# First stage of a two-layer LoRA network: products with gathered rows in four row quarters of the array

## The chip, the cores and the metric

One core of one Trainium2 chip runs the whole network as a single program. The metric is the device time of one execution in microseconds. It is 992.07 us before the change (median of 3 runs, 991.67 to 992.74).

## What is computed

The input x has 128 sequences of 32 tokens with 512 features, so 4,096 tokens. Two layers follow one another, each adding to x. The change lies in the first half of the first layer, a dense product with a low-rank correction (LoRA) whose factors are picked per sequence by a slot number:

```python
base_out = jnp.einsum('bti,oi->bto', x, W) + b
A = lora_As[adapter_mapping]          # per sequence, 512 x 16
Bm = lora_Bs[adapter_mapping]         # per sequence, 16 x 512
lora_h = jnp.einsum('bti,bir->btr', x, A)
lora_out = jnp.einsum('btr,bro->bto', lora_h, Bm)
return base_out + lora_out * SCALING
```

What it returns goes through a gated feed-forward block (gate, up and down weights with 1,376 hidden features), and the second layer is again of dense products with low-rank corrections. All arithmetic is in float32.

## The kernel before

**Arithmetic.** A float32 product is made of three products of a reduced type (`fp32r`): each operand is split into a high part (written by ACT) and a low part (the rest, written by DVE), and `mm3` (L1822) issues high x high, high x low and low x high into the same accumulator. Each of these is one weight load (128 columns) and one matmul.

**Stages.** Stage 1 (to about 149 us of the span) makes the output c of the code above in 8 tiles (`t`, NT = 8) of 512 tokens, and stores it to a scratch tensor. Stage 2 (to about 782 us) is the feed-forward block, and the rest is the second layer. The engines run programs written out by hand, each in a fixed order, and wait for each other on semaphores. PE's program for stage 1 is at the end of `pe_program`.

**One tile of stage 1 on PE.** The 512 output features are four blocks of 128 (`m`), each with a PSUM bank `acc[m]` of 128 features x 512 tokens. The 512 input features are four blocks (`k`).
- `cond_base(t, m, k)` is the dense product of block k into bank m: three matmuls over 512 tokens. A tile has 16 of them.
- `turn_a(t)` transposes the gathered factors A: a tile has 16 sequences in two groups (`g`, NG = 2) of 8 sequences, that is of 8 x 16 = 128 gathered rows and 256 tokens. Eight transposes go into two banks of the ring. ACT and DVE split them into `a_hi` and `a_lo` (`turn_a` of their programs, L955 and L1396).
- `lora_in(t)` multiplies x by them, 24 matmuls of 256 tokens, into one ring bank with 128 rows (sequence, rank). DVE masks the result (`h_masked`, L1410: `own_batch` leaves, of each sequence's 16 rows, only its own 32 tokens), ACT makes `lh_hi` (L967), and DVE `lh_lo` (L1416).
- `cond_lora(t, m)` multiplies the masked rows by the gathered factors B (`b_hi`, `b_lo`) and adds to bank m: for each of the two groups three matmuls with all 128 rows over 256 tokens. It closes the bank: its last matmul counts `pe_acc` up by one, ACT's `close_c` (L973) adds the bias, writes `c_out` and counts `c_closed`, and the next tile's first product into that bank waits for this.

The order on PE in tiles 1 to 7 is: base of bank 0, `turn_a`, base of bank 1, `lora_in`, base of banks 2 and 3, then `cond_lora` of banks 0 to 3. In tile 0 the dense products go block by block as the weights arrive, `lora_in` stands ahead of the last four of them, and the rest is the same.

**Around it.** In a tile ACT works in this order: `a_hi`, `b_hi`, `xa_hi` of the next tile, `lh_hi`, then four times `close_c` with a piece `dt` of the down weights behind it (tiles 0 to 5), or splits of the operands of stage 2 (`cop`, tiles 6 and 7). DVE's order is `a_lo`, `b_lo`, `xa_lo` of the next tile, `h_masked`, `lh_lo`, `dt` or `cop` work. Stage 2 begins with products into banks 0 and 2, which wait for `c_closed` of tile 7; behind them a product waits for ACT's copy of a bank (L1041).

Of the kernel before, what the change touches and what calls it, by code (L numbers as in the profile page):

```python
# [10 lines left out]
P = 128  # L11
# [13 lines left out]
def plain(ap):  # L25
    return ap.bitcast(F32)


def build(nc, x, slots, langs, w0, b0, ab_table, w_gate, w_up, w_down, wb1, rhs2, ra1, b2t, b1, out):
    NT, KC, _, _ = x.shape  # L30
# [8 lines left out]
    GT = GB * SEQ  # L39
    NG = TOK // GT  # L40
    E = P // R
# [54 lines left out]
    w0_hi = work("w0_hi", [KC, D], F32R)  # L96
# [193 lines left out]
    warm_done = sem("warm_done")  # L290
# [37 lines left out]
    def nth(t, m=KC - 1):  # L328
        return t * KC + m + 1
# [1045 lines left out]
    def dve_program(e):  # L1375
# [287 lines left out]
        e.memset(plain(warm[:, :]), 0.0).then_inc(warm_done, 1)  # L1663
# [154 lines left out]
    def pe_program(e):  # L1818
# [41 lines left out]
        def cond_base(t, m, k):  # L1860
            mm3(acc[m][:, :], w0_hi[:, k, m * P:(m + 1) * P], w0_lo[:, k, m * P:(m + 1) * P],
                xa_hi[t % 2][:, k, :], xa_lo[t % 2][:, k, :], k == 0, False)

        def cond_lora(t, m):
            s = t % 2
            for g in range(NG):
                tok = slice(g * GT, (g + 1) * GT)
                done = mm3(acc[m][:, tok], b_hi[s][:, g, m * P:(m + 1) * P], b_lo[s][:, g, m * P:(m + 1) * P],
                           lh_hi[s][:, tok], lh_lo[s][:, tok], False, g == NG - 1)
            done.then_inc(pe_acc, 1)  # L1870
# [188 lines left out]
        e.wait_ge(warm_done, 1)  # L2059
        for _ in range(9):  # L2060
            mm(ring[3][:, :], warm[:, 0:P], warm[:, :], True, True)
        for k in range(KC):
            e.wait_ge(x_lo, nth(0, k))
            e.wait_ge(w0_lo_done, k + 1)
            if k == 2:
                turn_a(0)
            if k == 3:
                lora_in(0)
            for m in range(KC):
                cond_base(0, m, k)  # L2070
        for t in range(NT):
            for m in range(KC):
                if t > 0:
                    e.wait_ge(c_closed, nth(t - 1, m))
                    for k in range(KC):
                        if m == 0:
                            e.wait_ge(x_lo, nth(t, k))
                        cond_base(t, m, k)
                    if m == 0:
                        turn_a(t)  # L2080
                    if m == 1:
                        lora_in(t)
            e.wait_ge(lh_lo_done, t + 1)
            e.wait_ge(b_lo_done, NG * (t + 1))
            for m in range(KC):
                cond_lora(t, m)
# [131 lines left out]
```

## Time and profile before

| | us |
|---|---|
| median of 3 runs | 992.07 (991.67 to 992.74) |
| profiled execution, its own time | 994.31 |
| its span | 992.6 |
| PE busy, share of the span | 982.7, 99% |
| DVE, ACT, POOL busy | 586.8, 464.9, 256.0 |
| DMA, mean over the span | 232 GB/s |

The span runs from the first to the last instruction. The profiled execution took 994.31 us, 2.2 us above the median of the runs shown. PE's busy time says little by itself, because a matmul's record is longer than the distance to the next one; the rows are read by the starts of neighbouring instructions.

### The profile page before, as it was taken

To read this page: it belongs to the slowest core of one execution; us is meant where nothing else is said; L and a number is where in the kernel's file an instruction comes from. 1 tells how busy PE (TensorE), PEld (TensorE's weight loads), DVE (VectorE), ACT (ScalarE), POOL (GpSimd) and SP (SyncE) were. 2 spreads that over 40 slices of the span, in tenths; PEclk is the share of its full clock that TensorE was granted. 3 is DMA by queue.
4 is the path that set the end of the run, shared out by engine and by line. 5 is a ranking of instruction groups with operands and counts; after the bars stand their busy time and mean duration, and the time that the engine had idled before them with its cause. 6 is when DMAs were issued, how large, how long until landed. Compare 5 with 4: busy or idle time off the path is not lost.

```text
span 992.6 us, 14042 instructions
## 1 busy us (share of the span) xinstructions
PE 982.7 (99%) x4787; PEld 830.4 (84%) x4787; DVE 586.8 (59%) x969; ACT 464.9 (47%) x854; POOL 256.0 (26%) x244
## 2 busy tenths in 40 slices
PE   9999999999999999999999999999999999999998
PEld 7888888878888888888888888888888998888876
DVE  5654586777784323596423398333377587785762
ACT  4645567555661333572333373233356273535342
POOL 5242232654400631400532230261140450000000
PEclk9999999999999999999999999999999999999999
DMA  8997866666977877867887777986688740615222
GB/s 287 334 327 281 309 216 245 240 231 236 340 265 260 283 229 193 274 222 267 287 278 193 233 249 248 321 279 192 192 293 285 254 166 28 228 61 194 78 93 85
DMA packets 121486, 230.12 MB, mean 232 GB/s; under 512 B 12612, under 2 KB 12612, under 8 KB 121160
## 3 DMA queue, kind: packets, MB, share of 16 engines
q1 hardware_dynamic: 118880, 220.81, 66.5%
q0 software_dynamic: 2400, 8.41, 2.3%
q8 instruction: 39, 0.64, 0.3%
q14 instruction: 31, 0.25, 0.1%
q10 hardware_dynamic: 136, 0.01, 0.0%
HBM read 165.74 MB, written 63.44 MB: 231 GB/s over the span
## 4 chain that ended last, share of the span: by engine, by line
PE 96%; DVE 1%; ACT 1%; issue 1%; DMA 0%; SPq 0%; ACTq 0%; DVEq 0%
PE bank L1820 95%; PE bank L1844 1%; PE bank L1981 1%; DMA w_raw<-in_w 0%; ACT xs_hi L1126 0%; ACT bank L1277 0%; DVE hg L1644 0%; DVE t_lo L1535 0%; DVE greater L1624 0%; ACT res L1285 0%; DVE diff L1601 0%; DVE top L1597 0%; DVE wins L1620 0%; DVE rank L1627 0%; DVE greater L1618 0%
## 5 line engine op out<-in xcount | busy, mean ns | idle before, releaser
L1820 PE MATMUL bank<-cop_hi,wring 128*128 128x512 f32 x1234 | 380.8, 389 | 0.9 <-ACT bank L1041 0.9
L1820 PEld LDWEIGHTS bank<-cop_hi,wring 128*128 128x128 f32 x1234 | 231.8, 188 | 49.4 <-ACT bank L1041 1.3
L1820 PE MATMUL bank<-cop_lo,wring 128*128 128x512 f32 x616 | 239.8, 389 | 0.0
L1820 PE MATMUL bank<-op_hi,wring 128*128 128x512 f32 x560 | 173.8, 389 | 0.0
L1472 DVE TENSOR_TENSOR v<-bank,p7s 128x512 f32<-128x512 f32 x44 | 30.4, 692 | 204.6 <-PE bank L1820 204.6
L1820 PEld LDWEIGHTS bank<-cop_lo,wring 128*128 128x128 f32 x616 | 115.7, 188 | 23.8
L1820 PEld LDWEIGHTS bank<-op_hi,wring 128*128 128x128 f32 x560 | 105.2, 188 | 21.7
L1820 PE MATMUL bank<-op_lo,wring 128*128 128x512 f32 x280 | 109.0, 389 | 0.0
L1072 ACT ACTIVATE s<-bank 128x512 f32<-128x512 f32 x44 | 26.3, 598 | 117.9 <-PE bank L1820 117.8
L1458 DVE TENSOR_TENSOR op_lo<-h,op_hi 128x512 fp32r<-128x512 f32 x100 | 72.9, 747 | 3.3 <-ACT op_hi L1029 3.1
L821 POOL TENSOR_TENSOR h_t<-h,h 128x512 f32<-128x512 f32 x20 | 27.7, 1385 | 161.1 <-DVE h L1494 161.1
L1029 ACT ACTIVATE op_hi<-h 128x512 fp32r<-128x512 f32 x100 | 62.7, 627 | 13.6 <-PE bank L1820 12.7
L1820 PEld LDWEIGHTS bank<-op_lo,wring 128*128 128x128 f32 x280 | 52.6, 188 | 10.9
L1041 ACT ACTIVATE bank<-bank 128x512 f32<-128x512 f32 x44 | 25.6, 582 | 76.7 <-PE bank L1820 76.7
L860 POOL TENSOR_TENSOR t_sum<-x_second,x_second 128x256 f32<-128x256 f32 x12 | 8.9, 780 | 177.3 <-DMA x_second<-x_scratch 177.3
L1820 PE MATMUL bank<-xa_hi,w_hi 128*128 128x512 f32 x128 | 51.6, 404 | 0.8 <-DVE w_lo L1389 0.8
L1820 PE MATMUL bank<-xa_lo,w_hi 128*128 128x512 f32 x128 | 50.8, 397 | 0.0
L1820 PE MATMUL bank<-xa_hi,w_lo 128*128 128x512 f32 x128 | 50.5, 395 | 0.0
L1477 DVE TENSOR_TENSOR p7s<-bank,p7s 128x512 f32<-128x512 f32 x44 | 30.4, 691 | 25.0 <-PE bank L1820 24.9
L1063 ACT ACTIVATE s<-bank 128x512 f32<-128x512 f32 x44 | 26.3, 599 | 30.6 <-PE bank L1820 30.6
L1048 ACT ACTIVATE p7s<-bank 128x512 f32<-128x512 f32 x44 | 26.3, 598 | 29.9 <-PE bank L1820 29.9
L776 POOL DMA_INDIRECT ab<-in_ab_table,row_i x16 | 18.7, 1171 | 81.9 <-DVE b_lo L1400 75.8
(227 smaller groups left out, 1931.4 us busy)
## 6 DMA issues: line engine op xcount, KB each, us to landing
wring<-wgu_scratch SPq DMA_DIRECT2D x231, 256.0 KB, 3.1
wring<-wd_scratch SPq DMA_DIRECT2D x140, 256.0 KB, 4.9
wgu_scratch<-wring SPq DMA_DIRECT2D x77, 256.0 KB, 3.5
x_raw<-in_x SPq DMA_DIRECT2D x32, 256.0 KB, 6.2
c_scratch<-c_out SPq DMA_DIRECT2D x32, 256.0 KB, 2.9
c<-c_scratch SPq DMA_DIRECT2D x32, 256.0 KB, 4.6
xs_raw<-x_scratch SPq DMA_DIRECT2D x16, 512.0 KB, 6.2
out<-res SPq DMA_DIRECT2D x32, 256.0 KB, 2.1
```

What stands on the lines that cost most here:

```text
L776: e.indirect_dma_start(out=ab[g][:, :], out_offset=None, in_=ab_table, in_offset=bass.IndirectOffsetOnAxis(ap=row_i[:, col:col + 1], axis= ...
L821: e.tensor_tensor(h_t3[p][:, :], h22[p][:, :], h12[p][:, :], ALU.subtract).then_inc(t3_done, 1)
L1029: e.activation(op_hi[n % N_OP][:, :], op_source[i][p][:, :], ACT.Copy).then_inc(op_hi_done, 1)
L1041: e.activation(bank_y[b][:, :], bank_a[b][:, :], ACT.Copy).then_inc(ay_done, 1)
L1048: e.activation(p7s[b][:, :], bank_w[b][:, :], ACT.Copy).then_inc(p7s_done, 1)
L1063: e.activation(s1[j % 2][:, :], bank_a[j % 2][:, :], ACT.Silu).then_inc(silu1_done, 1)
L1072: e.activation(s2[j % 2][:, :], bank_z[j % 2][:, :], ACT.Silu).then_inc(silu2_done, 1)
L1458: e.tensor_tensor(op_lo[n % N_OP][:, :], op_source[i][p][:, :], plain(op_hi[n % N_OP][:, :]), ALU.subtract).then_inc(op_lo_done, 1)
L1472: e.tensor_tensor(v[b][:, :], bank_z[b][:, :], p7s[b][:, :], ALU.add).then_inc(gc22_done, 1)
L1477: e.tensor_tensor(p7s[b][:, :], bank_y[b][:, :], p7s[b][:, :], ALU.add).then_inc(gc21_done, 1)
L1820: return e.matmul(out_ap, lhs, rhs, start=start, stop=stop, skip_group_check=True)
L1844: done = e.transpose(bank[:, k * P:(k + 1) * P], ab[g][:, k * P:(k + 1) * P], ident[:, :])
```

## The change

The mask leaves most of `cond_lora`'s products zero: of the 128 rows of a group, the 32 rows of a quarter (two sequences) meet only their own 64 tokens. The changed `cond_lora` multiplies only these. One matmul of 128 rows by 256 tokens becomes four of 32 rows by 64 tokens, each on its own quarter of the array's rows. The four that stand in a row write to four different banks: in turn 0 quarter i writes to bank i, in turn 1 to bank i + 1 and so on, and after four turns each quarter has been in each bank. A tile has 4 turns x 2 groups x 3 products x 4 quarters = 96 small matmuls. A turn waits, by the new semaphore `pe_turn`, until the turn before is complete, and three dense matmuls (`cond_base` of block k = 3) stand between two turns. All four banks close together, at the end of the last dense product, which counts `pe_acc` up by four. `turn_a` moves to the tile's head, and `lora_in` to just before bank 3 (in tile 0 all four last dense products, which stood behind `lora_in`, are now among the turns). The warm-up's semaphore is replaced by `dve_chain`, to make room for `pe_turn`.

```diff
+    PART = 32
+    NPART = P // PART
+    PT = GT // NPART
...
-    warm_done = sem("warm_done")
+    pe_turn = sem("pe_turn")
...
-        e.memset(plain(warm[:, :]), 0.0).then_inc(warm_done, 1)
+        linked(e.memset(plain(warm[:, :]), 0.0))
...
-            mm3(acc[m][:, :], w0_hi[:, k, m * P:(m + 1) * P], w0_lo[:, k, m * P:(m + 1) * P],
-                xa_hi[t % 2][:, k, :], xa_lo[t % 2][:, k, :], k == 0, False)
-
-        def cond_lora(t, m):
-            s = t % 2
-            for g in range(NG):
-                tok = slice(g * GT, (g + 1) * GT)
-                done = mm3(acc[m][:, tok], b_hi[s][:, g, m * P:(m + 1) * P], b_lo[s][:, g, m * P:(m + 1) * P],
-                           lh_hi[s][:, tok], lh_lo[s][:, tok], False, g == NG - 1)
-            done.then_inc(pe_acc, 1)
+            return mm3(acc[m][:, :], w0_hi[:, k, m * P:(m + 1) * P], w0_lo[:, k, m * P:(m + 1) * P],
+                       xa_hi[t % 2][:, k, :], xa_lo[t % 2][:, k, :], k == 0, k == KC - 1)
+
+        def cond_lora(t, turn):
+
+
+            s, own = t % 2, KC // NPART
+            if turn == 0:
+                e.wait_ge(lh_lo_done, t + 1)
+                e.wait_ge(b_lo_done, NG * (t + 1))
+            else:
+                e.wait_ge(pe_turn, (NPART - 1) * t + turn)
+            for c in range(own):
+                for g in range(NG):
+                    for b_, h_ in ((b_hi[s], lh_hi[s]), (b_hi[s], lh_lo[s]), (b_lo[s], lh_hi[s])):
+                        for i in range(NPART):
+                            m = (i + turn) % NPART * own + c
+                            rows, tok = slice(i * PART, (i + 1) * PART), slice(g * GT + i * PT, g * GT + (i + 1) * PT)
+                            done = mm(acc[m][:, tok], b_[rows, g, m * P:(m + 1) * P], h_[rows, tok], False, False)
+            if turn + 1 < NPART:
+                done.then_inc(pe_turn, 1)
...
-        for k in range(KC):
-            e.wait_ge(x_lo, nth(0, k))
-            e.wait_ge(w0_lo_done, k + 1)
-            if k == 2:
-                turn_a(0)
-            if k == 3:
-                lora_in(0)
-            for m in range(KC):
-                cond_base(0, m, k)
         for t in range(NT):
-            for m in range(KC):
-                if t > 0:
+            if t == 0:
+                for k in range(KC):
+                    e.wait_ge(x_lo, nth(0, k))
+                    e.wait_ge(w0_lo_done, k + 1)
+                    if k == 2:
+                        turn_a(0)
+                    if k == KC - 1:
+                        lora_in(0)
+                    else:
+                        for m in range(KC):
+                            cond_base(0, m, k)
+            else:
+                turn_a(t)
+                for m in range(KC):
                     e.wait_ge(c_closed, nth(t - 1, m))
-                    for k in range(KC):
+                    if m == KC - 1:
+                        lora_in(t)
+                    for k in range(KC - 1):
                         if m == 0:
                             e.wait_ge(x_lo, nth(t, k))
                         cond_base(t, m, k)
-                    if m == 0:
-                        turn_a(t)
-                    if m == 1:
-                        lora_in(t)
-            e.wait_ge(lh_lo_done, t + 1)
-            e.wait_ge(b_lo_done, NG * (t + 1))
-            for m in range(KC):
-                cond_lora(t, m)
+
+            cond_lora(t, 0)
+            for m in range(KC - 1, 0, -1):
+                cond_base(t, m, KC - 1)
+                cond_lora(t, KC - m)
+            cond_base(t, 0, KC - 1).then_inc(pe_acc, KC)
```

Where the order on PE moves (names with numbers are buffers; in the shapes, the columns are those of the output). First place, tile 0, from the last products of `lora_in` on. Before:

```order
L1820 MATMUL bank<-xa_hi_68,a_lo 128x256
L1820 MATMUL bank<-xa_hi_68,w_hi 128x512
L1820 MATMUL bank<-xa_lo_70,w_hi 128x512
L1820 MATMUL bank<-xa_hi_68,w_lo 128x512
L1820 MATMUL bank<-xa_hi_68,w_hi 128x512
L1820 MATMUL bank<-xa_lo_70,w_hi 128x512
L1820 MATMUL bank<-xa_hi_68,w_lo 128x512
```

Six more such dense matmuls follow, then `cond_lora`'s first, with its wait for `lh_lo_done`. Changed, the same place:

```order
L1824 MATMUL bank<-xa_hi_68,a_lo 128x256
L1824 MATMUL bank<-lh_hi_64,b_hi_60 128x64 x4
L1824 MATMUL bank<-lh_lo_66,b_hi_60 128x64 x4
L1824 MATMUL bank<-lh_hi_64,b_lo_62 128x64 x4
L1824 MATMUL bank<-lh_hi_64,b_hi_60 128x64 x4
L1824 MATMUL bank<-lh_lo_66,b_hi_60 128x64 x4
L1824 MATMUL bank<-lh_hi_64,b_lo_62 128x64 x4
L1824 MATMUL bank<-xa_hi_68,w_hi 128x512
```

The twelve dense matmuls that stood between `lora_in` and the products that need its result have moved behind the first of them.

Second place, tile 1, the end of `lora_in` and the first turns, with the waits. In the kernel before, `lora_in` is followed by 24 dense matmuls (banks 2 and 3). Changed, nine are left:

```order
162 L1824 MATMUL bank<-xa_hi_69,w_hi 128x512
...
170 L1824 MATMUL bank<-xa_hi_69,w_lo 128x512
171 L1824 MATMUL bank<-lh_hi_65,b_hi_61 128x64 [waits b_lo_done,lh_lo_done]
172 L1824 MATMUL bank<-lh_hi_65,b_hi_61 128x64 x3
173 L1824 MATMUL bank<-lh_lo_67,b_hi_61 128x64 x4
174 L1824 MATMUL bank<-lh_hi_65,b_lo_63 128x64 x4
175 L1824 MATMUL bank<-lh_hi_65,b_hi_61 128x64 x4
176 L1824 MATMUL bank<-lh_lo_67,b_hi_61 128x64 x4
177 L1824 MATMUL bank<-lh_hi_65,b_lo_63 128x64 x4
178 L1824 MATMUL bank<-xa_hi_69,w_hi 128x512
179 L1824 MATMUL bank<-xa_lo_71,w_hi 128x512
180 L1824 MATMUL bank<-xa_hi_69,w_lo 128x512
181 L1824 MATMUL bank<-lh_hi_65,b_hi_61 128x64 [waits pe_turn]
```

Third place, the border between tiles 0 and 1. Before, the products of `cond_lora` that close bank 3 are followed at once by the dense products of tile 1, whose first waits for `c_closed` of bank 0. Changed:

```order
104 L1824 MATMUL bank<-xa_hi_68,w_hi 128x512
105 L1824 MATMUL bank<-xa_lo_70,w_hi 128x512
106 L1824 MATMUL bank<-xa_hi_68,w_lo 128x512
107 L1848 MATMUL bank<-ident,ab_54 128x128 [waits ab_in0]
108 L1848 MATMUL bank<-ident,ab_54 128x128 x3
109 L1848 MATMUL bank<-ident,ab_55 128x128 [waits dve_freed,ab_in1]
110 L1848 MATMUL bank<-ident,ab_55 128x128 x3
111 L1824 MATMUL bank<-xa_hi_69,w_hi 128x512 [waits x_lo,c_closed]
```

The eight transposes have moved ahead of the first dense product, between the closing of the four banks and the wait for the first of them. On DVE, ACT, POOL and SP the order is the same in both kernels.

## Rows read from the trace of the kernel before

**Rows 1.** The page: busy time, the chain that ended last, one costly group.
```profile
PE 982.7 (99%) x4787; PEld 830.4 (84%) x4787; DVE 586.8 (59%) x969; ACT 464.9 (47%) x854; POOL 256.0 (26%) x244
...
PE bank L1820 95%; PE bank L1844 1%; PE bank L1981 1%; DMA w_raw<-in_w 0%; ACT xs_hi L1126 0%; ACT bank L1277 0%; DVE hg L1644 0%; DVE t_lo L1535 0%; DVE greater L1624 0%; ACT res L1285 0%; DVE diff L1601 0%; DVE top L1597 0%; DVE wins L1620 0%; DVE rank L1627 0%; DVE greater L1618 0%
...
L1820 PE MATMUL bank<-xa_hi,w_hi 128*128 128x512 f32 x128 | 51.6, 404 | 0.8 <-DVE w_lo L1389 0.8
```

The last of these reads: count, busy us, mean ns of one, idle us of PE just before them and what ended it.

**Rows 2.** Chain of waits in stage 1, tile 1: start us, us, what.
```profile
28.86 0.87 PE bank L1844 x8
29.73 16.73 PE bank L1820 x96
```

**Rows 3.** Timeline of PE, tile 1: start us, us, engine, line, op, tile.
```profile
35.21 0.40 PE L1820 MATMUL bank<-xa_hi,w_hi 128*128 128x512 f32 x1
...
40.45 0.39 PE L1820 MATMUL bank<-xa_hi,w_lo 128*128 128x512 f32 x1
40.67 0.28 PE L1820 MATMUL bank<-lh_hi,b_hi 128*128 128x256 f32 x1
...
43.43 0.28 PE L1820 MATMUL bank<-lh_hi,b_lo 128*128 128x256 f32 x1
43.55 0.40 PE L1820 MATMUL bank<-xa_hi,w_hi 128*128 128x512 f32 x1
```

**Rows 4.** Weight loads and matmuls by tile: duration ns min/median/max, first and last start.
```profile
L1820 PEld LDWEIGHTS bank<-warm x9: 287/330/333, 1.5 to 4.7; 128*128 128x128 f32 x9
L1820 PE MATMUL bank<-warm x9: 628/628/794, 1.5 to 5.1; 128*128 128x512 f32 x9
L1820 PEld LDWEIGHTS bank<-cop_hi,wring x1234: 186/188/192, 149.0 to 728.3; 128*128 128x128 f32 x177
```

**Rows 5.** Timeline of PE, tile 0, the first matmul behind `lora_in`.
```profile
20.31 0.40 PE L1820 MATMUL bank<-xa_hi,w_hi 128*128 128x512 f32 x1
```

**Rows 6.** Timeline of DVE, tiles 0 and 1.
```profile
20.51 0.69 DVE L1410 SCALAR_TENSOR_TENSOR h_masked<-bank,own_batch 128x512 f32<-128x512 f32 x1 [1.72 <-PE bank L1820]
21.90 0.94 DVE L1416 TENSOR_TENSOR lh_lo<-h_masked,lh_hi 128x512 fp32r<-128x512 f32 x1 [0.70 <-ACT lh_hi L967]
...
29.96 1.29 DVE L1396 TENSOR_TENSOR a_lo<-bank,a_hi 128x512 fp32r<-128x512 f32 x2 [0.82 <-ACT a_hi L955]
...
32.37 2.49 DVE L1385 TENSOR_TENSOR xa_lo<-x_raw,xa_hi 128x512 fp32r<-128x512 f32 x4
35.41 0.69 DVE L1410 SCALAR_TENSOR_TENSOR h_masked<-bank,own_batch 128x512 f32<-128x512 f32 x1 [0.55 <-PE bank L1820]
36.80 0.69 DVE L1416 TENSOR_TENSOR lh_lo<-h_masked,lh_hi 128x512 fp32r<-128x512 f32 x1 [0.70 <-ACT lh_hi L967]
```

**Rows 7.** Chain of waits, second layer: what a long wait of PE ended with.
```profile
958.46 0.69 DVE res L1552
```

**Rows 8.** Timeline of PE at the same place.
```profile
959.19 0.50 PE L1820 MATMUL bank<-t_hi,s_hi 128*128 128x512 f32 x1 [1.93 <-DVE res L1552]
959.53 0.40 PE L1820 MATMUL bank<-t_lo,s_hi 128*128 128x512 f32 x1
959.76 0.40 PE L1820 MATMUL bank<-t_hi,s_lo 128*128 128x512 f32 x1
```

**Rows 9.** Timeline of ACT, tile 1.
```profile
41.59 0.69 ACT L973 ACTIVATE c_out<-bank,b 128x512 f32<-128x512 f32 x1 [4.82 <-PE bank L1820]
...
45.44 0.64 ACT L1000 ACTIVATE dt<-ds 128x512 fp32r<-128x512 f32 x1
```

**Rows 10.** Timeline of DVE, tiles 6 and 7.
```profile
124.73 1.15 DVE L1416 TENSOR_TENSOR lh_lo<-h_masked,lh_hi 128x512 fp32r<-128x512 f32 x1 [0.70 <-ACT lh_hi L967]
...
141.38 0.69 DVE L1436 TENSOR_TENSOR c_t<-c,c 128x512 f32<-128x512 f32 x1 [1.03 <-DMA c<-c_scratch]
```

**Rows 11.** Timeline of ACT, start of stage 2.
```profile
149.88 1.14 ACT L1014 ACTIVATE cop_hi<-c 128x512 fp32r<-128x512 f32 x2
150.92 0.59 ACT L1041 ACTIVATE bank<-bank 128x512 f32<-128x512 f32 x1
```

More of the change, by code:

```diff
@@ L2057, in out_h2 @@
                 False, True).then_inc(pe_acc, 1)
-        e.wait_ge(warm_done, 1)
+        e.wait_ge(dve_chain, 1)
         for _ in range(9):
             mm(ring[3][:, :], warm[:, 0:P], warm[:, :], True, True)
-        for k in range(KC):
-            e.wait_ge(x_lo, nth(0, k))
-            e.wait_ge(w0_lo_done, k + 1)
-            if k == 2:
-                turn_a(0)
-            if k == 3:
-                lora_in(0)
-            for m in range(KC):
-                cond_base(0, m, k)
-        for t in range(NT):
-            for m in range(KC):
-                if t > 0:
+        for t in range(NT):
+            if t == 0:
[12 more added lines that the diff above has]
+                for m in range(KC):
                     e.wait_ge(c_closed, nth(t - 1, m))
-                    for k in range(KC):
+                    if m == KC - 1:
+                        lora_in(t)
+                    for k in range(KC - 1):
                         if m == 0:
```

## The prediction

> **What bounds the kernel.** I read the page first: PE is busy 99% of the span, and its matmuls make 95% of the chain that ended last [rows 1]. Before the 128 first products of the dense blocks, all of them in stage 1, PE idled 0.8 us, once, for the first weights [rows 1]. The chain of waits says the same of one tile: eight transposes (0.87 us) and 96 matmuls (16.73 us), and nothing between [rows 2]. So a tile takes 17.60 us without a wait, and two things count: what PE no longer streams, and what PE now waits for. Third I read PE's timeline by its starts. Dense matmuls of 512 columns start about 0.227 us apart (24 of them from 35.21 to 40.67), those of 256 columns 0.120 us apart, and the 24 of `cond_lora` take 43.55 - 40.67 = 2.88 us a tile [rows 3], 23.0 us in 8 tiles. That is all that the change can win. It would need PE not to lose it elsewhere. Last I read ACT and DVE for what feeds `cond_lora`.
>
> **The small matmuls.** Removed: 24 matmuls of 256 columns, 2.88 us a tile. Added: 96 of 64 columns and 32 rows, in 24 rounds of four. No such instruction is in the trace, so their price is bounded. From the two distances [rows 3] 256 columns cost 0.107 us and a matmul 0.013 us on top; four at once, bound by their columns alone, would be 64 columns and one fixed part, 0.027 + 0.013 = 0.040 us a round, 0.96 us a tile. At the other end nothing overlaps. The nearest row to a short matmul with a load of its own is a transpose, 128 columns, eight in 0.87 us or 0.109 us each [rows 2]; 96 of those are 10.4 us a tile. Between these ends I ask what a weight load takes. Its record is 330 ns while the matmul's is 628 and 188 when that is about 389 [rows 3, 4], so it gives back 142 ns where the matmul of 512 columns gives back 239. Half the clock costs 512 columns 213 ns; some 26 ns of the 239 are other than columns, and the load has 142 - 26 = 116 ns of array time when fast (an estimate from these rows), as if its 128 columns went through twice. So behind a matmul of 256 columns the load is just covered, and behind one of 64 columns it isn't. If the loads of the four quarters run side by side, a round takes one load, about what a 256-column matmul takes now. I take 0.120 us a round: 24 x 0.120 = 2.88 us, **no gain at all**, with 0.96 and 10.4 us as ends.
>
> The Trainium skill (TensorE: Matmul & The Clock Gate, LDWEIGHTS) says that a load takes its columns divided by 1.2 in ns, and that 32 rows by 128 columns take as long as 128 by 128. By that, an estimate, a round is 0.107 us and the kernel would stand 2.5 us lower than my sum.
>
> **Changing between quarters and whole array.** A tile has four turns, so eight changes, 64 in all. A dense matmul's record is 0.39 us against a distance of 0.227 us [rows 3]: 0.16 us of each lies under its successor. If this overlap is lost at a change, it costs 0.16 us; if not, nothing. Eight first changes fall into the wait below. I take 56 x 0.16 = **+9.0 us**, with 0 as the other end. This is the second thing that no row shows.
>
> The Trainium skill (TensorEngine Tiling, Key Properties) has a rule against the change here: changing the tiling mode drains the array. It gives no price; by it 0.16 us stands, without it the sum is 9.0 us less.
>
> **The wait for `lh_lo`.** `lora_in`'s result goes through DVE, ACT, DVE. In tile 0 the next matmul after `lora_in` starts at 20.31 [rows 5], and `lh_lo` ends at 21.90 + 0.94 = 22.84 [rows 6]. Twelve dense matmuls (2.72 us) covered this, and now stand behind it. A wait costs some 0.14 us beyond its releaser: DVE's `res` ended at 959.15 [rows 7], PE's next record began at 959.19, and the distance to the one behind it was 0.34 us in place of 0.227 [rows 8]. So PE stands still 2.53 + 0.14 = **+2.7 us**, once. In tiles 1 to 7 nine dense matmuls are left, 2.04 us. From the start behind `lora_in` (35.21) to the end of `lh_lo` (37.49) are 2.28 us [rows 3, 6]: 0.24 + 0.14, and some 0.05 us more because DVE itself is only just ready. With T as the end of the tile before on PE's stream: ACT closes four banks with four `dt` in about 4.5 us [rows 9], DVE's `a_lo` can start at T + 5.3 (one `a_hi` lies between), from there to its last `xa_lo` are 4.9 us [rows 6], so DVE is free at T + 10.2; PE ends `lora_in` at T + 9.95 (0.87 + 6.12 + 2.88, and 0.1 from below). I count 0.45 us for tiles 1 to 5, **+2.3**; 0.9 for tile 6, where `lh_lo` took 1.15 us and not 0.69; and 1.3 for tile 7, where DVE waits for a transfer first [rows 10]: **+2.2**.
>
> **Banks that close together.** The closing starts 0.2 us after T and takes 0.69 us [rows 9], so bank 0 is free at T + 0.9. The transposes, moved ahead, cover 0.87 us of it: 0.1 us at each of 7 borders, **+0.7**. The other banks are freed before PE asks, 2 us apart. At the start of stage 2 no transposes stand there: **+1.0**. There ACT also makes two `cop_hi` (1.14 us) between the closings and the copy that the third product waits for [rows 11]. They end at T + 3.8, the copy at T + 4.4, PE asks at T + 3.75: **+0.7**. `pe_turn` costs nothing: the three dense matmuls between (0.68 us) cover the 0.28 us that a record takes.
>
> The transposes need only their gathered rows, asked for a tile ahead. DMA, POOL and SP have the same list and slack.
>
> **Sum.** 0 (small matmuls) + 9.0 (changes) + 2.7 + 2.3 + 2.2 + 0.7 + 1.0 + 0.7 (waits, 9.6) = +18.6 us. The profiled execution goes from a span of 992.6 to 1011.2. It took 994.31 us, 2.2 above the median; on the median of 992.07 the forecast is 1010.7, **1011 us**.
>
> **Rival A: the quarters run side by side and their loads are short.** If a load of 32 rows takes a quarter of a full one, or several are held ready, a round is 0.040 us and a tile saves 2.88 - 0.96 = 1.92 us, 15.4 in 8. Less waits of 9.6: -5.8, 986 us if changes cost nothing, and 995 us with them. This is the case on the faster side. It decides at 0.070 us a round with free changes. For it: the four of a round use other rows and other banks. Against it: the load record in [rows 4]. The Trainium skill (TensorEngine Tiling, Key Properties) says that different tiles load and multiply in parallel; no row here shows it, and by it either the forecast or this rival holds.
>
> **Rival B: the quarters don't overlap.** Each small pair costs what a transpose costs, 0.109 us. Then 96 x 0.109 = 10.5 us a tile in place of 2.88, +60.7 in all, and with the waits +70: 1062 us, 1071 with the changes. For it: the transposes, the shortest pairs there are, stand no closer than 0.109 us [rows 2]. Against it: none there had another quarter to go to. This is also the case in which the change doesn't do what it says.
>
> **Rival C: PE falls to its slow clock in the wait of tile 0.** Matmul records of 628 ns mark it [rows 4]. Against it: after 1.93 us of idling the next record was 0.50 us, with 0.40 behind it [rows 8], so the fast level held. It would add some us and change no sign; I fold it into the others.
>
> **Chances.** Forecast, a round between 0.09 and 0.20 us and all in all 1000 to 1030 us: 0.50. Rival A: 0.27, of it 0.22 faster, 0.03 no difference, 0.02 slower. Rival B: 0.23. Two in a thousand, 2 us, is about what a measurement can tell from no change. So faster 0.22, same 0.04 (0.01 from the forecast's edge), slower 0.74. The forecast's case alone spans 1000 to 1030. The range reaches down to rival A with free changes, 985, and up to rival B without them, 1063; what lies above 1063 and some of A below 985 is left out, about 0.2.
>
> **What would show it.** In the changed profile: starts of the 128x64 matmuls 0.03 us apart on average (rival A: 0.01, rival B: 0.11); a turn of 24 taking 0.7 us and the distance to the dense matmul behind it 0.16 longer than its pattern; PE waiting once for 2.5 us or so for DVE L1420 in tile 0 and about 0.4 in the others, and for ACT L977 at the borders. Tiles would be 17.6 + 1.1 + 0.6 = 19.3 us. The prediction is wrong if a turn takes below 0.3 us or above 2 us, or if the wait for `lh_lo` doesn't show.

## The result, and the profile after

| | before | changed |
|---|---|---|
| median of 4 runs each | 992.40 us (991.67 to 994.35) | **1024.01 us** (1021.68 to 1025.88) |
| profiled execution, its own time | 994.31 | 1021.68 |
| its span | 992.6 | 1020.0 |

The ratio is 1.0316 (1.0292 to 1.0341): the change costs 3.2%, 31.6 us on the medians and 27.4 us between the two profiled spans. The forecast was 1011 us. The sign and the range held, its own case (no gain at all from the small matmuls) is what came, and 13 us are missing from its sum on the medians, 8.8 us between the profiled spans (1011.2 against 1020.0).

The page of the changed kernel, with the lines that answer to [rows 1], and the row of PE's granted clock:

```profile
span 1020.0 us, 15201 instructions
PE 1004.0 (98%) x5363; PEld 836.0 (82%) x5363; DVE 586.9 (58%) x969; ACT 463.3 (45%) x854; POOL 255.3 (25%) x244
...
PEclk9799997999999999999999999999999999999999
```

576 matmuls more than in [rows 1], still 98% busy, and two slices of the 40 (each 25.5 us) at about three quarters of the clock. The kernel before has a mean granted clock of 1.000 in its profiled execution, the changed one 0.987. Cut at the places where the dense matmuls change their pace (columns: window, length, PE, PEld, DVE, ACT, POOL busy with counts, granted clock, DMA share, GB/s):

```profile
23.00:37.00 14.00, 14.00 (x99) 10.75 (x98) 2.54 (x4) 4.18 (x8) 4.49 (x4) 0.51 0.61 235
37.00:164.00 127.00, 123.43 (x1110) 100.69 (x1108) 66.21 (x107) 60.14 (x118) 31.69 (x28) 1.00 0.75 266
166.00:181.00 15.00, 14.22 (x97) 10.47 (x94) 7.48 (x15) 6.13 (x14) 4.32 (x4) 0.54 0.25 91
181.00:1020.00 839.00, 832.30 (x3932) 698.24 (x3930) 495.72 (x823) 379.41 (x696) 203.97 (x188) 1.00 0.68 221
```

There are two stretches at about half clock (the 1.2 GHz level), in windows of 14 and 15 us, and the other two windows have a granted clock of 1.00 (the 2.4 GHz level). Each begins just behind the two long waits for `lh_lo`, in tile 0 and in tile 7. PE's timeline in tile 0:

```profile
21.75 0.30 PE L1824 MATMUL bank<-lh_hi,b_hi 32*128 32x64 f32 x4 [2.17 <-DVE lh_lo L1420]
...
23.10 0.59 PE L1824 MATMUL bank<-xa_hi,w_lo 128*128 128x512 f32 x1
...
24.07 0.40 PE L1824 MATMUL bank<-lh_hi,b_lo 32*128 32x64 f32 x4
24.29 0.40 PE L1824 MATMUL bank<-lh_hi,b_hi 32*128 32x64 f32 x4
...
36.76 0.42 PE L1824 MATMUL bank<-xa_hi,w_hi 128*128 128x512 f32 x1
```

A dense record grows from 0.39 to 0.6 us and a round of four from 0.11 to 0.21 us (24.07 to 24.29). The first slow dense record starts 1.35 us after the wait ended (21.75 to 23.10), the first fast one again at 36.76, 13.7 us later.

**One turn at full clock**, in tile 1. First PE, then its weight loads:

```profile
48.15 0.40 PE L1824 MATMUL bank<-xa_hi,w_lo 128*128 128x512 f32 x1
48.47 0.30 PE L1824 MATMUL bank<-lh_hi,b_hi 32*128 32x64 f32 x4
48.61 0.28 PE L1824 MATMUL bank<-lh_lo,b_hi 32*128 32x64 f32 x4
...
49.05 0.28 PE L1824 MATMUL bank<-lh_hi,b_lo 32*128 32x64 f32 x4
49.26 0.50 PE L1824 MATMUL bank<-xa_hi,w_hi 128*128 128x512 f32 x1
49.60 0.39 PE L1824 MATMUL bank<-xa_lo,w_hi 128*128 128x512 f32 x1
```

```profile
48.47 0.19 PEld L1824 LDWEIGHTS bank<-lh_hi,b_hi 32*128 32x128 f32 x4 [0.36 <-issue]
48.58 0.19 PEld L1824 LDWEIGHTS bank<-lh_lo,b_hi 32*128 32x128 f32 x4
```

The four of a round are so close that the view shows them as one row ("x4"), matmuls and loads alike, and the next four follow 0.11 us later. So the quarters do run side by side, and a round still takes 0.112 us, about what the forecast gave one load (0.116), against the 0.120 us of the 256-column matmul that it replaces [rows 3]. The edges can be read off too: dense to quarter 0.32 us (48.15 to 48.47) where dense to dense is 0.227, the first round 0.14, quarter to dense 0.21 (49.05 to 49.26), and then 0.34 to the second dense matmul. Over the undisturbed distances (0.227 and 0.112) that is 0.12 us on the way to the quarters and 0.21 us on the way back.

**One tile**, by the chain of waits in tiles 2 and 3 (answers to [rows 2]):

```profile
65.09 0.72 DVE lh_lo L1420
...
65.86 6.82 PE bank L1824 x108
```

`lh_lo` stands on the path in every tile now, where the chain before had matmuls alone. And what PE waited for, in all (us, times, longest):

```profile
PE bank L1824 <- DVE lh_lo L1420: 5.3, 3, 2.6
```

The list of waits shows idle time only beyond a matmul's record, which is why five tiles with a shorter wait are not in it. In starts:

```profile
65.34 0.39 PE L1824 MATMUL bank<-xa_hi,w_lo 128*128 128x512 f32 x1
65.86 0.30 PE L1824 MATMUL bank<-lh_hi,b_hi 32*128 32x64 f32 x4
```

These are 0.52 us in place of 0.227: 0.29 us more (0.26 to 0.29 in the five tiles), of which some 0.09 us are the change to the quarters, which costs as much where nothing is waited for (0.32 above).

### The profile page after: what moved, and what is told of

Its sections match the earlier page's. It is cut to its first block, busy times and chain, and to the rows that moved or that the text cites. A ratio compares the mean times of both kernels' runs of the same rounds, so it can differ in the third digit from the quotient of the medians.

```text
span 1020.0 us, 15201 instructions
## 1 busy us (share of the span) xinstructions
PE 1004.0 (98%) x5363; PEld 836.0 (82%) x5363; DVE 586.9 (58%) x969; ACT 463.3 (45%) x854; POOL 255.3 (25%) x244
## 4 chain that ended last, share of the span: by engine, by line
PE 92%; DVE 3%; ACT 2%; DMA 1%; issue 1%; POOL 0%; SPq 0%; ACTq 0%; DVEq 0%
PE bank L1824 90%; DMA ab<-in_ab_table,row_i 1%; PE bank L1996 1%; PE bank L1848 1%; DVE lh_lo L1420 1%; DVE h_masked L1414 1%; ACT lh_hi L971 1%; DMA c<-c_scratch 0%; ACT xs_hi L1130 0%; ACT c_out L977 0%; DMA slot_i<-in_slots 0%; DVE xa_lo L1389 0%; DVE cop_lo L1448 0%; ACT dt L1004 0%; ACT bank L1281 0%
## 5 line engine op out<-in xcount | busy, mean ns | idle before, releaser
L1076 ACT ACTIVATE s<-bank 128x512 f32<-128x512 f32 x44 | 26.3, 597 | 116.7 <-PE bank L1824 116.7
L1824 PE MATMUL bank<-xa_hi,w_hi 128*128 128x512 f32 x128 | 56.9, 444 | 1.1 <-DVE w_lo L1393 1.0
L977 ACT ACTIVATE c_out<-bank,b 128x512 f32<-128x512 f32 x32 | 21.1, 687 | 63.3 <-PE bank L1824 63.3
```

Source lines behind the costliest of these rows:

```text
L977: e.activation(c_out[m][:, :], acc[m][:, :], ACT.Identity, bias=b0_sb[:, m:m + 1]).then_inc(c_closed, 1)
L1076: e.activation(s2[j % 2][:, :], bank_z[j % 2][:, :], ACT.Silu).then_inc(silu2_done, 1)
L1824: return e.matmul(out_ap, lhs, rhs, start=start, stop=stop, skip_group_check=True)
```

## The experiments

The theory after the result: the rounds and edges cost what the forecast says, and the rest of the loss is half clock, brought on by waits that now stand beside small matmuls. Rivals: the columns bound the round and not the load; the quarters alone bring the slow clock; the waits alone bring it. There are nine runs, of eight kernels and the changed one again, in three groups, each beside the kernel before on the same chip: 992.08 us (991.53 to 996.22, 7 runs) in the first, 994.25 (991.66 to 995.71, 7 runs) in the second, 994.68 (one run) in the third. "Clock" is the mean granted clock of a run. The kernel before is not free of the low level either: of these fifteen runs of it seven have a clock of 1.000 (991.53 to 994.25 us) and eight one of 0.998 (993.49 to 996.22 us).

**wide** (first group). Each quarter multiplies all 256 tokens of its group; the added columns are the mask's zeros.

```diff
-                            rows, tok = slice(i * PART, (i + 1) * PART), slice(g * GT + i * PT, g * GT + (i + 1) * PT)
+                            rows, tok = slice(i * PART, (i + 1) * PART), slice(g * GT, (g + 1) * GT)
```

> Each small matmul takes all 256 tokens of its group in place of its quarter's 64 (the added products are zero, so the result is the same). Loads set the round: four streams side by side, a round goes from 0.112 to 0.120 us, a turn from 0.67 to about 0.72 us, the kernel is 1 to 2 us over the changed one. Rival, the four streams run one behind another (4 x 64 columns are 0.107 us too): a round takes 4 x 0.107 = 0.43 us, a turn 2.6 us, the kernel some 60 us more.

Measured: 1019.5 us (one run), clock 0.995. PE's timeline:

```profile
64.36 0.39 PE L1824 MATMUL bank<-lh_hi,b_hi 32*128 32x256 f32 x4
64.58 0.28 PE L1824 MATMUL bank<-lh_lo,b_hi 32*128 32x256 f32 x4
...
65.28 0.50 PE L1824 MATMUL bank<-xa_hi,w_hi 128*128 128x512 f32 x1
```

Four times the columns, and a round takes 0.120 us instead of 0.112: four streams of 256 columns pass side by side in the time of one. Only the first round of a turn grows (0.22 in place of 0.14), so a turn costs 0.92 us instead of 0.79, some 4 us over 32 turns. The time falls nevertheless, since the two slow phases shrink, from 13.6 us each to 3.4.

**narrow** (third group). The opposite: half of the tokens, 32 columns. It leaves the correction of the other half out.

```diff
-                            rows, tok = slice(i * PART, (i + 1) * PART), slice(g * GT + i * PT, g * GT + (i + 1) * PT)
+                            rows, tok = slice(i * PART, (i + 1) * PART), slice(g * GT + i * PT, g * GT + i * PT + PT // 2)
```

> Each quarter's matmul takes 32 of its 64 tokens (the correction of the other half of the tokens is left out). If the round is one weight load, it stays at 0.112 us and a turn at 0.79 us, for a quarter of what a load hides now; the time is that of the changed kernel or, with longer slow phases, a few us more: 1022 to 1030 us. Rival, columns or the pace at which instructions are issued set part of the round: by columns a round falls below 0.10 us, 1.5 us or more off the eight tiles.

Measured: 1022.5 us (one run), clock 0.987, the changed kernel's time. PE's timeline:

```profile
67.88 0.27 PE L1824 MATMUL bank<-lh_hi,b_lo 32*128 32x32 f32 x4
67.99 0.27 PE L1824 MATMUL bank<-lh_hi,b_hi 32*128 32x32 f32 x4
```

Half the columns, the same 0.112 us. At 32 and 64 columns something other than columns is the bound, and the load, which is 32 x 128 in both and in flight all the time, is the candidate. The other one, a pace of issuing four pairs of instructions a round, is excluded by the next run, where two pairs take as long. No run varied the columns of the load itself.

**halves** (second group). Two halves of 64 rows by 128 tokens, in two turns: as many rounds in a tile (24), half the edges.

```diff
-    PART = 32
+    PART = 64
...
-            for m in range(KC - 1, 0, -1):
+            for m in range(KC - 1, 1, -1):
                 cond_base(t, m, KC - 1)
-                cond_lora(t, KC - m)
-            cond_base(t, 0, KC - 1).then_inc(pe_acc, KC)
+            cond_lora(t, 1)
+            for m in (1, 0):
+                done = cond_base(t, m, KC - 1)
+            done.then_inc(pe_acc, KC)
```

> Two halves of 64 rows and 128 tokens in place of four quarters, two turns of 24 matmuls with two banks a half, six dense matmuls between. Loads set the round: a round of two takes 0.112 us still, 24 rounds a tile as before, so only the edges change, four a tile in place of eight: 32 x 0.167 = 5.4 us less, 1004 us without slow phases. With twice the columns per round slow phases are shorter: 1005 to 1012 us. Rival, the round goes by the columns streamed: 128 columns take 0.067 us, a tile gains 1.1 us more, below 1000 us.

Measured: 1013.92 us (1011.75 to 1018.73, 4 runs), 1.0209 (1.0171 to 1.0248), clocks 0.988 to 0.995; above the 1005 to 1012 expected. One tile, with a round of two halves:

```profile
60.11 0.33 PE L1824 MATMUL bank<-lh_hi,b_hi 64*128 64x128 f32 x2
...
61.27 0.28 PE L1824 MATMUL bank<-lh_lo,b_hi 64*128 64x128 f32 x2
61.39 0.28 PE L1824 MATMUL bank<-lh_hi,b_lo 64*128 64x128 f32 x2
...
66.13 1.08 PE L1848 MATMUL bank<-ident,ab 128*128 128x128 f32 x8
```

0.112 us again, now with twice the rows, twice the columns and half the instructions. If the load sets it, a load takes the same with 32 rows as with 64. The halved edges show in the trace: from the first half to the transposes are 6.02 us (60.11 to 66.13), where the changed kernel has 6.66, so 0.6 us a tile or some 5 us in eight are gained, as expected (5.4). The other half of the gain on after_again's 1024.42 us is less slow clock (below), but not as little of it as expected.

**whole_rows** (first group). The changed kernel's order, waits and closings, with the old products of 128 rows by 256 tokens in the turns. It is everything but the quarters.

```diff
-            for c in range(own):
-                for g in range(NG):
-                    for b_, h_ in ((b_hi[s], lh_hi[s]), (b_hi[s], lh_lo[s]), (b_lo[s], lh_hi[s])):
-                        for i in range(NPART):
-                            m = (i + turn) % NPART * own + c
-                            rows, tok = slice(i * PART, (i + 1) * PART), slice(g * GT + i * PT, g * GT + (i + 1) * PT)
-                            done = mm(acc[m][:, tok], b_[rows, g, m * P:(m + 1) * P], h_[rows, tok], False, False)
+            for g in range(NG):
+                tok = slice(g * GT, (g + 1) * GT)
+                done = mm3(acc[turn][:, tok], b_hi[s][:, g, turn * P:(turn + 1) * P], b_lo[s][:, g, turn * P:(turn + 1) * P],
+                           lh_hi[s][:, tok], lh_lo[s][:, tok], False, False)
```

> Order, waits and semaphores of the changed kernel, but with the old products of 128 rows and 256 tokens, one bank a turn. The changes of row mode cost: no loss at the edges of a turn, 10.6 us go (64 x 0.167), 1.5 us come (rounds of 0.120). If idling alone starts the slow phases they stay, and the time is 1013 to 1016 us; if it takes the row quarters too, 1001 us. Rival, the edges cost because of the wait for pe_turn and not of the row mode: the loss of 0.17 us an edge stays, 1022 us or more.

Measured: 1005.99 us (1004.24 to 1006.50, 4 runs), 1.0129 (1.0101 to 1.0157), clocks 0.997 and 0.998. Neither expected value: the edges are gone, and so is nearly all of the slow clock. One tile in its timeline:

```profile
76.34 0.38 PE L1824 MATMUL bank<-lh_hi,b_hi 128*128 128x256 f32 x1
...
82.08 1.03 PE L1848 MATMUL bank<-ident,ab 128*128 128x128 f32 x8
```

From the first product of the correction to the transposes are 5.74 us; 12 x 0.227 + 24 x 0.120 = 5.60, and 0.10 of the rest is the first matmul behind a wait. The same stretch in the changed kernel runs from 65.86 to 72.52, 6.66 us, with rounds of only 0.112. It has 5.41 + 1.25 us, where whole_rows, with the same waits for `pe_turn`, has almost nothing over. So the 1.25 us are the seven changes between quarters and whole array, **0.18 us each** on average: three of 0.12 us to the quarters and four of 0.21 us back. It is not the short columns: in wide, with 256 columns as here, the same stretch takes 7.14 us, so its changes cost no less. What whole_rows still loses (11.5 us between the profiled spans) is the waits, the borders, the start of stage 2 and a little slow clock.

Its wait in tile 7:

```profile
152.07 0.39 PE L1824 MATMUL bank<-lh_hi,b_hi 128*128 128x256 f32 x1 [2.62 <-DVE lh_lo L1420]
```

And windows of this kernel (columns as above; the granted clock is the third number from the end), the first around the wait in tile 0, which is 2.17 us long as in the changed kernel:

```profile
19.00:30.00 11.00, 8.44 (x53) 7.22 (x52) 3.28 (x5) 4.33 (x8) 5.05 (x4) 1.00 1.00 377
...
153.00:157.00 4.00, 4.00 (x18) 3.52 (x17) 3.90 (x5) 0.89 (x2) 2.62 (x3) 0.57 0.05 16
```

After the 2.62 us of waiting the clock does fall, 1.28 us later (the dense matmul at 153.35 has a record of 0.63 us), but from 156.7 it is full again. After the 2.17 us it doesn't fall at all.

**filler** (first group). Ten dense matmuls, whose result nobody reads, fill the two long waits.

```diff
+            if t in (0, NT - 1):
+                for _ in range(10):
+                    mm(ring[3 if t == 0 else 0][:, :], w0_hi[:, 0, 0:P], xa_hi[t % 2][:, 0, :], True, True)
             cond_lora(t, 0)
```

> As the changed kernel, with ten dense matmuls of 512 columns into an unused bank in the two long waits for lh_lo (tiles 0 and 7). The idle time starts the slow phases: all matmul records stay at 0.39 us after the first 10 us, and 13 us of the 31 go: 1010 to 1013 us. Rival, the row quarters themselves keep the array too little occupied: the slow phases stay and the time is 1021 to 1026 us.

Measured: 1015.26 us (1010.08 to 1017.00, 4 runs), 1.0211 (1.0170 to 1.0251), clocks 0.995, 0.995, 0.993 and 1.000. Half of what was expected. The two phases are gone, 9 us with them, but in the profiled run another came in tile 4:

```profile
100.00:114.00 14.00, 13.74 (x123) 10.79 (x124) 1.72 (x5) 3.90 (x9) 0.80 (x1) 0.63 0.44 167
```

```profile
100.26 0.30 PE L1824 MATMUL bank<-lh_hi,b_hi 32*128 32x64 f32 x4 [0.56 <-DVE lh_lo L1420]
```

A wait of 0.56 us stands ahead of it, where `lh_lo` took longer than elsewhere; the changed kernel has the same wait there (0.54 us) and no slow phase behind it. The one run with a clock of 1.000 took 1010.08 us, 18.0 above the kernel before beside it: the forecast's sum (18.6) without a slow clock.

**wide_filler** (second group): both edits.

> Both remedies: ten dense matmuls in the two long waits, and 256 columns in each quarter's matmul. If a low occupancy of the array (waits, and quarters of 64 columns) makes the slow phases, there are none, in any run: granted clock 1.000, and the time is the changed kernel's without slow phases (1009) plus 32 turns x 0.13 us for the wider rounds: 1013 us, with a narrow scatter. Rival, row quarters as such (their mode, or their idle edges) bring the slow clock: phases like those of the filler run appear, 1016 us or more, scattered.

Measured: 1016.46 us (1013.87 to 1017.15, 4 runs), 1.0217 (1.0191 to 1.0242), and a clock of 1.000 in all four, where filler alone had it in one of four. Over the kernel before beside it that is 22.2 us: the 18.0 of filler's fast run and the 4.2 that 32 turns of 0.92 instead of 0.79 us cost. Most of stage 1:

```profile
13.00:100.00 87.00, 86.48 (x759) 69.97 (x758) 42.08 (x63) 40.05 (x74) 24.30 (x19) 1.00 0.78 276
```

The added columns, each of them a product with zero, came with a full clock; they cost about what they save here.

**cover** (first group). In tiles 0 and 7 the last dense products come first and cover the wait, and the four turns follow in a row; from tile 1 on `lora_in` stands six dense matmuls earlier.

```diff
-                    if m == KC - 1:
-                        lora_in(t)
                     for k in range(KC - 1):
...
+                        if m == KC - 2 and k == 1:
+                            lora_in(t)
                         cond_base(t, m, k)
...
+            if t in (0, NT - 1):
+                for m in range(KC):
+                    cond_base(t, m, KC - 1)
+                for turn in range(NPART):
+                    done = cond_lora(t, turn)
+                done.then_inc(pe_acc, KC)
+            else:
```

> Row quarters as in the changed kernel, lora_in six dense matmuls earlier in tiles 1 to 7, and in tiles 0 and 7 all dense products ahead of the turns, so that nothing waits for lh_lo. Left of the loss: 48 changes in tiles 1 to 6 (8.0), 2 changes and 3 exposed turn waits in tiles 0 and 7 (about 1.2 each), borders and the start of stage 2 (1.7), less 1.5 for shorter rounds: 1003 us, with no slow phase. If the row quarters start the slow phases: 1010 us or more.

Measured: 1010.67 us (1008.85 to 1012.72, 4 runs), 1.0183 (1.0152 to 1.0215), clocks 0.993 to 0.995. Better than the changed kernel, but 8 us above what was expected. No wait for `lh_lo` is left, and yet there are two slow phases, from 27.5 and from 164.0 us, behind the turns in a row:

```profile
28.91 1.11 PE L1848 MATMUL bank<-ident,ab 128*128 128x128 f32 x4 [1.33 <-DMA ab<-in_ab_table,row_i]
```

Having no dense products left between the turns, PE is early at the next tile and waits for the gathered rows, from 27.6 us on, when the clock has just fallen (in together, below, it falls at 26.0 us and this wait begins at 26.9). The chain of waits in tile 7 shows what a turn costs without a dense product behind it (start us, us, what):

```profile
161.68 0.89 PE bank L1824 x24
...
162.61 0.89 PE bank L1824 x24
```

0.93 us from turn to turn: six rounds of 0.112 and 0.26 us for the wait on the end of the turn before. With dense products between the turns it costs nothing that whole_rows would show.

**together** (second group): cover's order in all tiles (`if t >= 0`).

> Row quarters, nothing waits for lh_lo, all dense products of a tile ahead of its four turns, in every tile. A turn costs 0.93 us (as in tile 7 of the cover run), so a tile's turns 3.7 and two edges in place of 2.88: +1.0 a tile, 8; with borders and stage 2's start 1003 us. If sparse turns in a row (3.7 us of 64-column quarters) are enough to bring the slow clock, phases appear in most tiles and the time is 1010 to 1040 us.

Measured: 1013.63 us (1013.23 to 1014.73, 4 runs), 1.0199 (1.0177 to 1.0222), clocks 0.987 in three runs and 0.988. This was to show whether the quarters need a wait to bring the slow clock. They don't. PE's timeline in tile 3:

```profile
83.44 0.30 PE L1824 MATMUL bank<-lh_hi,b_hi 32*128 32x64 f32 x4
...
87.03 1.63 PE L1848 MATMUL bank<-ident,ab 128*128 128x128 f32 x8
88.31 0.77 PE L1824 MATMUL bank<-xa_hi,w_hi 128*128 128x512 f32 x1
```

Four turns in 3.6 us, no wait recorded on PE from 80 to 90 us, a granted clock of 1.2 GHz from 87.4 us on, and the transposes behind them already take 1.28 us (87.03 to 88.31) in place of 0.94 at full clock (the changed kernel's from 72.52 to 73.46).

**after_again** (second group): the changed kernel once more, in the group of halves and together.

> The changed kernel once more, beside the next three. 1020 to 1026 us, with slow phases of 10 us and more that begin in tiles 0 and 7 behind the long waits, or now and then elsewhere in stage 1; a run's time is 1008 to 1010 us plus its share of slow clock (1 - granted clock) times its time.

Measured: 1024.42 us (1022.93 to 1029.02, 4 runs), 1.0317 (1.0282 to 1.0353), clocks 0.980 to 0.987. The result repeats, the number of phases doesn't quite: the profiled run (1024.14 us) has a third one, from 145.6 to 155.8 us.

**Where the clock is low, in all of them.** The stretches in which the granted clock of the profiled run is at the 1.2 GHz level, in us, from windows of 1 us over the whole span:

| kernel | what is special | slow phases | in all |
|---|---|---|---|
| changed | | 23.1–36.8, 166.5–180.1 | 27.2 |
| after_again | same kernel | 22.7–36.4, 145.6–155.8, 169.5–183.1 | 37.5 |
| narrow | 32 columns | 24.5–38.2, 167.9–181.6 | 27.4 |
| filler | long waits filled | 103.2–113.4 | 10.2 |
| wide | 256 columns | 7.9–11.4, 25.0–28.4, 165.0–168.4 | 10.2 |
| wide_filler | both | none | 0 |
| halves | 64 rows | 22.8–26.2, 155.9–166.2, 978.5–981.9 | 17.0 |
| whole_rows | 128 rows | 153.3–156.7 | 3.4 |
| cover | turns in a row in tiles 0 and 7 | 27.5–34.3, 164.0–167.4 | 10.2 |
| together | turns in a row everywhere | 26.0–32.8, five of 3.4 us to 169.4, 978.3–981.7 | 27.2 |

The kernel before has none within its span. Some of these phases have nothing to do with the change: that of wide at 7.9 us stands ahead of the first quarter, and those of halves and together at 978 us are in the second layer, whose order no kernel here touches. There PE waits as in [rows 8], with dense matmuls on both sides:

```profile
977.00 0.50 PE L1824 MATMUL bank<-t_hi,s_hi 128*128 128x512 f32 x1 [1.91 <-DVE res L1556]
```

In halves the first record of 0.6 us follows at 978.51. In the other profiled runs the clock stays full there.

Read together: an empty wait can bring the low clock on with whole-array products behind it (whole_rows in tile 7, halves and together in the second layer), and a stretch of 64-column quarters can without an idle stretch ahead of it (together, in six of its eight tiles). Neither does so each time. With both it came each time: behind the long wait of tile 0 in all five profiles that have quarters or halves after it, and not in whole_rows. together has as much slow clock in all as the changed kernel, in shorter pieces (its turns still wait 0.26 us for each other, which the profile doesn't list as idle), so turns in a row are a cause nearly as large as the two combined. How long a phase stays goes with what PE does meanwhile. Where turns of 64- or 32-column quarters stand between the dense products it lasts 10 to 14 us, through the rest of the turns and the transposes; with 256 columns or whole rows it lasted 3.4 us, and with halves 3.4 us once and 10.2 us once.

## Why the prediction came out as it did

The terms of its sum, against the profiled executions:

| term | forecast | measured |
|---|---|---|
| small matmuls, 8 x 24 rounds | 0 (0.120 a round) | -1.5 (0.112) |
| changes, 56 | +9.0 (0.16 each) | +9.9 (0.18) |
| waits for `lh_lo` | +7.2 | +7.1 |
| of it tile 0 / tile 7 | 2.7 / 1.3 | 2.3 / 2.7 |
| 7 borders | +0.7 (0.1 each) | +1.4 (0.20) |
| start of stage 2 | +1.0 | +1.0 |
| ACT's copy behind it | +0.7 | 0 (0.4 at full clock) |
| slow clock | not in the sum | +11.3 |

**The small matmuls: right, and for the reason given, as far as the runs can tell.** The step that took 116 ns of array time for a load from the two record lengths in [rows 4] is the one that everything hung on. Measured is 0.112 us a round at 32 columns, at 64 and with halves at 128, and with two pairs of instructions as with four; the load is what stayed the same. Rival A (0.040 us) would have needed short loads, rival B (0.109 us for each small pair) quarters one after the other. By the rule of the Trainium skill (TensorE: Matmul & The Clock Gate, LDWEIGHTS), columns divided by 1.2 in ns whatever the rows are, a load takes 0.107 us, an estimate. The trace agrees within 5% (a round of 0.112 us with 32 rows and, in halves, with 64). That different tiles load and multiply in parallel (the Trainium skill, TensorEngine Tiling, Key Properties) agrees too: four pairs pass in 0.112 us.

**The changes: right, a little low.** 0.18 us in place of 0.16. whole_rows, beside wide, shows that it is the change between quarters and whole rows that costs it, and neither a wait nor the columns. The way it costs is not the forecast's: the first quarter starts 0.32 us behind a dense matmul whose record is 0.40 us, so part of the overlap is left, and the larger share is lost on the way back. The Trainium skill (TensorEngine Tiling, Key Properties) says that such a change drains the array; that it costs time agrees, but no row shows the array empty.

**The waits: right in sum, by luck in part.** Tile 7 waited twice as long as said (2.7 us for 1.3), and most of the others less. In tile 7 the path runs through the transfer of c: it is asked for behind DVE's last `cop_lo` (to 154.28 us), takes 4.85 us, and DVE stands 1.64 us for it, in place of 1.03 [rows 10], before it can mask `lora_in`'s result. In tiles 1, 2, 3, 5 and 6 it is 0.26 to 0.29 us each, not 0.45 (and 0.9 in tile 6). The slow `lh_lo` came in tile 4, with 0.70 us, and not in tile 6. First tile 7, from the chain of waits and DVE's timeline, then `lh_lo` in tile 4:

```profile
155.61 4.85 DMA c<-c_scratch
...
160.65 0.69 DVE L1440 TENSOR_TENSOR c_t<-c,c 128x512 f32<-128x512 f32 x1 [1.64 <-DMA c<-c_scratch]
```

```profile
103.25 1.12 DVE L1420 TENSOR_TENSOR lh_lo<-h_masked,lh_hi 128x512 fp32r<-128x512 f32 x1 [0.70 <-ACT lh_hi L971]
```

**The borders and the start of stage 2.** A border costs 0.20 us, twice what was said. At the start of stage 2 PE waits for the first closing as forecast; ACT's copy, which was to be late by 0.7 us more, shows 0.25 us of idling before it on ACT itself, so ACT was not the late one. That is the slow clock's doing: PE, at half its clock, asked later. In filler, which has the full clock there, PE does wait for the copy, and the start comes 0.60 us behind the one before (174.21 to 174.81) in place of 0.227, 0.4 us more. First the changed kernel, the closing and the copy, then filler:

```profile
175.04 0.80 PE L1824 MATMUL bank<-cop_hi,wring 128*128 128x512 f32 x1 [0.78 <-ACT c_out L977]
```

```profile
178.00 0.58 ACT L1045 ACTIVATE bank<-bank 128x512 f32<-128x512 f32 x1 [0.25 <-PE bank L1824]
```

```profile
174.81 0.50 PE L1824 MATMUL bank<-cop_hi,wring 128*128 128x512 f32 x1 [0.20 <-ACT bank L1045]
```

**The slow clock: the step that failed.** The prediction named it as rival C and let it go: "after 1.93 us of idling the next record was 0.50 us, with 0.40 behind it [rows 8], so the fast level held. It would add some us and change no sign; I fold it into the others." That row is a wait with dense matmuls of 512 columns and 128 rows behind it. Here it has quarters behind it, and a wait of 2.17 us was enough, where the same 2.17 us with whole-array products behind them (whole_rows) brought nothing. Nor was the row safe in its own place: behind the same wait the clock fell in halves and in together, so one execution in which it held proves little. And the price, "some us", was never worked out. It can be read by the same matmuls at both levels. From the last dense matmul between the first two turns to the seventh dense one of the next tile, tile 2 takes 7.73 us at full clock:

```profile
67.22 0.40 PE L1824 MATMUL bank<-xa_hi,w_lo 128*128 128x512 f32 x1
...
74.95 0.39 PE L1824 MATMUL bank<-xa_hi,w_hi 128*128 128x512 f32 x1
```

Tile 0 takes 13.66 us for them (23.10 to 36.76), 5.9 more. In tile 7 the last three dense groups with the two turns between them take 7.02 us (166.61 to 173.63) in place of 3.95 (68.34 to 72.29), 3.1 more, and the first eleven matmuls of stage 2 4.86 us in place of 2.52, 2.3 more: 11.3 us in all, for 27.2 us at the low level. Without them the profiled span would be 1008.7 us, and the forecast for it was 1011.2. filler's run at a clock of 1.000 (1010.08 us) says the same.

**What is not settled.** The measured column adds up to 29.2 us, and the spans differ by 27.4. Two things are gone that nobody forecast. Tile 0 comes to `lora_in` 0.9 us earlier (`lora_in` of tile 0 begins at 16.54 in place of 17.43): in the profiled run of the kernel before the first dense matmuls still have long records, to 10.1 us, and in that of the changed kernel they have short ones from the start. Before, then changed:

```profile
9.68 0.63 PE L1820 MATMUL bank<-xa_lo,w_hi 128*128 128x512 f32 x1
```

```profile
9.16 0.39 PE L1824 MATMUL bank<-xa_lo,w_hi 128*128 128x512 f32 x1
```

The view's granted clock reads 1.00 in both there. Four of the nine later runs (narrow, filler, wide_filler and cover) have the long records too, so this goes by the run and is no gain of the change. And a wait of 0.9 us for ACT, some 60 us into stage 2, has vanished. With both the sum is 27.4 us. Open is why a phase comes in one run and not in another (0.980 to 0.987 with the same kernel; in tile 4 once after a wait of 0.56 us), and what exactly ends it. An order in which the turns do not wait for each other was not tried. No kernel here beat the one before, and with rounds of 0.112 instead of 0.120 us all that is to be won is 1.5 us, against 9.9 for the edges alone.

## What to carry to other kernels

Before a matmul is cut into row quarters to skip zeros, look at what its weight load takes: where the matmul is about as long as its load, as a 256-column matmul here, fewer columns win nothing, and each change between quarters and whole array costs another 0.18 us. A row that dismisses a rival must have the same work around it, not only the same wait, and must be seen in more than one run: the clock held behind that wait in most profiles and fell in two. And price what you fold into the others, for the one term without a number (11.3 us) was larger than the whole error of the sum (8.8).

## What the runs showed of the hardware

- Four matmuls of 32 rows, 256 columns each, run side by side in 0.120 us, as one of 128 rows does; their four loads too. At 32 and 64 columns a round takes 0.112 us.
- Two halves of 64 rows and 128 columns also take 0.112 us.
- A change costs 0.12 us from the whole array to 64-column quarters and 0.21 us back; the same order with whole-array products has neither (whole_rows).
- Waiting for the end of one's own last matmul, with nothing between, costs 0.26 us more than going on.
- The granted clock fell without idle time ahead of it, behind turns of 64-column quarters in a row (3.6 us), in six tiles of together, but not in its tiles 1 and 5. With 256-column quarters and filled waits it was 1.000 in four runs of four.
- It also fell behind waits of 1.9 and 2.6 us with whole-array matmuls after them, in some profiles and not in others. 27.2 us at the low level cost the changed kernel 11.3 us.
